# Result stage of a selective-scan kernel in batches: eight weights-block matmuls, then eight 64-row state matmuls

## Chip, core and metric

One NeuronCore of a Trainium2 chip runs the whole program. The metric is the device time of one execution in microseconds (us), as the median of several runs. TensorE does matmuls and transposes, VectorE (DVE), ScalarE (ACT) and GpSimd (POOL) do the elementwise work, SyncE (SP) issues most DMAs and GpSimd the indexed ones. All data are 32-bit floats. The engines run side by side and wait for each other by semaphores.

## What is computed

The input x has 16 images of 256 channels by 32 x 32 = 1024 tokens. Two blocks are added to it. The first scales channels by a small gating network. The second, cut to what matters:

```python
xz = silu(in_proj_w @ gn(x) + in_proj_b)            # 768 rows: x_ssm, res, gate
xf = silu(conv1d_depthwise_3(x_ssm) + dw_b)
dbc = dbc_w @ xf + dbc_b                            # per head: dt, B (8), C (8)
x_h, dt, B_t, C_t = gather by perm[head]            # the head's own order of tokens
# for each token t, S = 8 states per channel:
h = exp(dt_t * A) * h + (dt_t * B_t) * x_t
y_t = sum_s h * C_t   + D * x_t
y = gather back; y = y * silu(gate) + res
x = x + silu(out_proj_w @ y + out_proj_b)
```

There are 2 heads of 128 channels.

## The kernel before

**Tiling and stages.** The images are taken two at a time (NB = 2), so there are PH = 8 phases, written as cycle(i, ...) on every engine. The tokens of a head are cut into 8 tiles of 128 (g = 0 to 7), each of 8 chunks of 16 tokens. The scan isn't run token by token. Inside a chunk it becomes a matmul with a 128 x 128 block of weights (mblk, one for each image and tile), and across chunks a short scan on VectorE gives the state in front of each chunk (hs). The result of a tile is a sum of two matmuls into one PSUM region: the weights block times the gathered rows (x_rows), contraction over 128 rows, here called the weights-block matmul; and the turned C factors times the turned states, contraction over the 64 rows of 8 chunks by 8 states, here called the state matmul.

**The result stage on TensorE.** results(i, h, ...) makes the result of head h for both images. It works in units k = 0 to 7, four for each image b, each of two tiles (e = 0 and 1). turn(i, h, k, ...) transposes cblk and hs for the two tiles at once into PSUM (tp), so that the first tile's state operands come to rows 0 to 63 and the second's to rows 64 to 127. ScalarE copies them to ch (four slots of two times 128 columns, line L570) and signals t_drained. result(i, h, k, ...) waits for that copy and issues four matmuls: weights-block (L1256) and state (L1258) of tile 0 into bank pj[2b], then the same of tile 1 into pj[2b + 1]. The turns run AHEAD = 2 units in front. In head 0 the chunk sums of head 1's first image (st, L1230) are called after unit 3 (between). An f32 matmul is recorded as two weight loads and two matmuls, so 16 + 16 matmuls of a call are 32 + 32 records.

**What stands around it.** TensorE, in a phase: gate matmuls, chunk sums of head 0, the projection of the next phase's first image (project, L1183), results of head 0, the second image's projection mixed with the next phase's rows (L1204, L1206), chunk sums of head 1's second image, results of head 1, rows of the next phase's second image with residual matmuls, turning back, output (L1304). ScalarE runs its own fixed order: turned(...) makes the copies to ch, result(...) copies four tiles per bank from pj to rs (L580) once ch_used says that an image's four units are done, and in head 1 the activation of xf (convolved, L526) stands between the rs copies of the first image and copies 6 and 7. VectorE makes cblk (L1030, after head 0's turns), the scans hs (L995), the weights blocks mblk (L1038 to L1049) and the convolution (L933). GpSimd weighs (L413), gathers head 0's result back in 8 indexed DMAs (L401, once all scans are done), scatters the next phase's rows (L389) and in between gathers head 1's. SyncE stores rs, loads the scattered rows, stores and loads the C rows, stores the output and loads x.

Of the kernel before, what the change touches and what calls it, by code (L numbers as in the profile page):

```python
# [23 lines left out]
P = 128  # L24
# [5 lines left out]
NB = 2  # L30
# [45 lines left out]
def build(nc, x_d, w1g_d, b1g_d, w2_d, b2_d, inw_d, inb_d, dww_d, dwb_d, dbcw_d, dbcb_d, alog_d,  # L76
          dpar_d, mob_d, outw_d, outb_d, const_d, out_d):
    with ExitStack() as ctx:
        def sb(name, width, dt=F32):
            return ctx.enter_context(nc.sbuf_tensor(name, [P, width], dt))  # L80
# [14 lines left out]


        cst = sb("cst", CONST_W)
        inw = sb("inw", CT * 3 * C)
# [19 lines left out]
        hs = sb("hs", NB * (NC + 1) * S)  # L118
        ch = sb("ch", 4 * 2 * P)
        gt = sb("gt", NB * CT * N)  # L120
# [81 lines left out]
        X_U, T_U, Y_U = NB * NT, H * NB * NT // 2, NB * H * 2  # L202
        CH = 4
        AHEAD = 2
# [917 lines left out]
        def _(pe):  # L1122
# [96 lines left out]
            def x_rows(h, b, g):  # L1219
                return v(xp, (h * NT + g) * ROW + b * P, (1, P))  # L1220
# [22 lines left out]

            def result(i, h, k, before):

                b, gp = divmod(k, 4)
                u = h * 8 + k

                if gp == 0:
                    pj_slot(2 * b + 1, None, None, before)  # L1250
                    pe.wait_ge(mblk_ready, i * H + h + 1)
                pe.wait_ge(t_drained, i * T_U + u + 1)
                for e in range(2):
                    g = 2 * gp + e
                    d = v(pj[2 * b + e], gp * P, (1, P))
                    nc.tensor.matmul(d, v(mblk, (b * NT + g) * P, (1, P)), x_rows(h, b, g), start=True, stop=False)  # L1256
                    half_rows = dict(parts=64, p0=64 * e)
                    last = nc.tensor.matmul(d, v(ch, (u % CH) * 2 * P, (1, P), **half_rows),  # L1258
                                            v(ch, (u % CH) * 2 * P + P, (1, P), **half_rows), start=False, stop=True)
                last.then_inc(ch_used, 1)  # L1260

            def results(i, h, before_t, before_r, turned_before=0, between=None):
                for k in range(turned_before, AHEAD):
                    turn(i, h, k, before_t)
                for k in range(8):
                    if k + AHEAD < 8:
                        turn(i, h, k + AHEAD, before_t)
                    result(i, h, k, before_r)
                    if k == 3 and between:
                        between()  # L1270

# [166 lines left out]
```

## Time and profile before

| | |
|---|---|
| median of 3 runs | 1252.72 us (1245.59 to 1258.89) |
| span of the profiled execution, first to last instruction | 1174.1 us |
| TensorE matmul busy | 961.5 us (82%), 3988 instructions |
| VectorE busy | 588.0 us (50%) |
| ScalarE busy | 579.1 us (49%) |
| GpSimd busy | 532.4 us (45%) |
| weights-block matmuls L1256 | 512 records, 120.1 us busy |
| state matmuls L1258 | 512 records, 129.2 us busy |
| mean granted clock of TensorE | 0.890 |

The times of the runs are whole executions; the profile covers one execution from its first to its last instruction, and the time of that execution itself isn't given. Busy time of TensorE counts a matmul from its start to its modelled end, and neighbours overlap, so what a matmul takes of the engine is better read from the distance between starts. The granted clock is 1.00 at 2.4 GHz and 0.50 at 1.2 GHz.

### The profile page before, as it was taken

The page shows a single profiled execution, that of the slowest core. Times are in us where ns is not written, and L with a number is a line of the kernel's source. Part 1 is how long each engine was busy: PE and PEld are TensorE (multiplying, and loading weights), DVE is VectorE, ACT ScalarE, POOL GpSimd, SP SyncE. Part 2 cuts the span into 40 slices and gives each one's busy share as a digit, 9 for nine tenths or more (in the row PEclk, how much of TensorE's full clock was granted, in tenths as well). Part 3 has the DMA queues.
Part 4 walks back from the last instruction along what each step waited for, and adds up shares of the span by engine and source line. Part 5 has one row for each costly group of instructions (what it writes and reads, how often), then busy time and mean ns, then how long its engine had stood idle before and what let it go on. Part 6 is the DMA issues. An engine that isn't in the chain of part 4 may idle for free.

```text
span 1174.1 us, 12950 instructions
## 1 busy us (share of the span) xinstructions
PE 961.5 (82%) x3988; PEld 597.9 (51%) x3988; DVE 588.0 (50%) x1104; ACT 579.1 (49%) x1078; POOL 532.4 (45%) x628
## 2 busy tenths in 40 slices
PE   1039666997899988998899779997999889978966
PEld 0035445664467445754476346744575357634643
DVE  5966136534572448444753348243853466345613
ACT  4824423345734564547444564456553754456341
POOL 0002527164555627371826545471936373644340
PEclk9558765798899998999899989998999899998987
DMA  8830290135912391247513491238313661348122
GB/s 331 331 120 1 81 157 1 36 119 155 216 36 93 101 226 71 72 133 183 140 37 121 144 213 48 78 101 192 121 63 122 179 162 37 119 152 148 37 94 86
DMA packets 112051, 142.54 MB, mean 121 GB/s; under 512 B 41705, under 2 KB 91122, under 8 KB 111986
## 3 DMA queue, kind: packets, MB, share of 16 engines
q1 hardware_dynamic: 99698, 105.91, 34.0%
q0 software_dynamic: 12288, 35.80, 9.4%
q8 instruction: 36, 0.59, 0.2%
q14 instruction: 29, 0.24, 0.1%
HBM read 88.07 MB, written 53.61 MB: 121 GB/s over the span
## 4 chain that ended last, share of the span: by engine, by line
PE 41%; DMA 21%; POOL 16%; issue 10%; DVE 5%; SPq 4%; ACT 3%; POOLq 0%; ACTq 0%; DVEq 0%
PE pj L1183 12%; POOL xt_scratch L389 10%; PE pj L1258 9%; PE pj L1256 8%; DMA xb<-in_x 7%; DMA cd_scratch<-xp 6%; POOL big L401 4%; SPq L302 4%; PE st L1230 3%; DMA xp<-xt_scratch 2%; DMA xt_scratch<-stage,idx 2%; PE tp L1241 2%; PE tp L1206 2%; DMA crow<-cd_scratch 2%; POOL big L413 2%
## 5 line engine op out<-in xcount | busy, mean ns | idle before, releaser
L1183 PE MATMUL pj<-xb,wsc 128*128 128x512 f32 x768 | 392.1, 658 | 39.0 <-DMA xb<-in_x 26.6
L413 POOL TENSOR_TENSOR big<-big,crow 128x128 f32<-128x128 f32 x256 | 182.1, 751 | 212.6 <-DMA crow<-cd_scratch 199.1
L1183 PEld LDWEIGHTS pj<-xb,wsc 128*128 128x128 f32 x768 | 155.0, 213 | 205.9 <-issue 197.7
L389 POOL DMA_INDIRECT xt_scratch<-stage,idx x128 | 139.6, 1091 | 83.0 <-DVE stage L941 46.4
L358 POOL TENSOR_SCALAR wsc<-inw,pcur 128x256 f32<-128x256 f32 x96 | 62.6, 669 | 239.1 <-PE pj L1183 150.7
L401 POOL DMA_INDIRECT big<-yt_scratch,idx x128 | 130.5, 1020 | 75.5 <-issue 37.7
L1258 PE MATMUL pj<-ch 64*128 64x128 f32 x512 | 129.2, 333 | 0.0
L1256 PE MATMUL pj<-xp,mblk 128*128 128x128 f32 x512 | 120.1, 318 | 4.2 <-ACT xs L519 4.2
L1304 PE MATMUL pj<-gt,outw 128*128 128x512 f32 x256 | 111.8, 594 | 0.1
L995 DVE TENSOR_TENSOR_SCAN hs<-big,st 128x64 f32<-128x64 f32 x256 | 49.0, 265 | 101.8 <-PE st L1230 101.8
L570 ACT COPY ch<-tp 128x256 f32<-128x256 f32 x128 | 45.4, 376 | 106.6 <-PE tp L1242 106.6
L1258 PEld LDWEIGHTS pj<-ch 64*128 64x128 f32 x512 | 78.6, 192 | 32.6 <-issue 3.6
L1256 PEld LDWEIGHTS pj<-xp,mblk 128*128 128x128 f32 x512 | 80.0, 197 | 25.1 <-ACT xs L519 4.6
L559 ACT COPY stage<-tp 128x256 f32<-128x256 f32 x128 | 48.0, 375 | 81.4 <-PE tp L1206 77.0
L933 DVE SCALAR_TENSOR_TENSOR xf<-xs,small,xf 128x1024 f32<-128x1024 f32 x64 | 86.1, 1356 | 3.1 <-POOL xf L425 1.4
L1059 DVE TENSOR_TENSOR gt<-tp,gt 128x512 f32<-128x512 f32 x64 | 41.7, 687 | 90.3 <-PE tp L1294 90.0
L941 DVE TENSOR_TENSOR stage<-stage,small 128x68 f32<-128x68 f32 x64 | 14.8, 231 | 134.4 <-ACT stage L560 133.4
L1304 PEld LDWEIGHTS pj<-gt,outw 128*128 128x128 f32 x256 | 48.2, 191 | 58.1 <-issue 57.7
L1230 PEld LDWEIGHTS st<-bblk,xp 128*128 128x128 f32 x512 | 66.0, 205 | 21.2 <-issue 20.1
L580 ACT COPY rs<-pj 128x512 f32<-128x512 f32 x64 | 34.4, 589 | 85.8 <-PE pj L1258 85.8
L1230 PE MATMUL st<-bblk,xp 128*128 128x64 f32 x512 | 66.9, 288 | 8.8 <-DVE bblk L1021 8.8
L547 ACT ACTIVATE big<-sg,small 128x400 f32<-128x400 f32 x128 | 63.9, 610 | 19.6 <-POOL big L413 16.9
(192 smaller groups left out, 1348.7 us busy)
## 6 DMA issues: line engine op xcount, KB each, us to landing
xb<-in_x SPq DMA_DIRECT2D x32, 1024.0 KB, 7.4
xp<-xt_scratch SPq DMA_DIRECT2D x8, 2048.0 KB, 10.0
crow<-cd_scratch SPq DMA_DIRECT2D x128, 128.0 KB, 7.8
yt_scratch<-rs SPq DMA_DIRECT2D x16, 1024.0 KB, 4.4
out<-xb SPq DMA_DIRECT2D x16, 1024.0 KB, 10.2
xp<-xt_scratch SPq DMA_DIRECT2D x8, 272.0 KB, 3.5
xt_scratch<-stage,idx POOLq DMA_INDIRECT x128
big<-yt_scratch,idx POOLq DMA_INDIRECT x128, 2.7
```

The costliest lines, as they stand in the source:

```text
L358: last = nc.gpsimd.tensor_scalar(v(wsc, (b * CT + ct) * 2 * C + slot * C, (1, C)), v(inw, ct * 3 * C + col, (1, C)), v(pcur, (par * NB + b ...
L389: pool.indirect_dma_start(out=xt_d.ap(), out_offset=bass.IndirectOffsetOnAxis(ap=idx[:, k:k + 1], axis=0), in_=v(stage, (nt * H + h) * ROW ...
L401: pool.indirect_dma_start(out=v(big, k * NB * P, (1, NB * P)), out_offset=None, in_=yt_d.ap()[0:(h + 1) * N], in_offset=bass.IndirectOffse ...
L413: last = nc.gpsimd.tensor_tensor(v(big, W_OFF + (s * Q + b * NT) * L, (L, NT), (1, L)), v(big, s * EEW + SEG + b * NT * L, (L, NT), (1, L) ...
L547: last = nc.scalar.activation(v(big, s * EEW, (1, EEW)), v(sg, 0, (1, EEW)), ACT.Exp, scale=v(small, ANEG + h * S + s, (1, 1)))
L933: nc.vector.scalar_tensor_tensor(dst, tap(k), wt(k), dst, ALU.mult, ALU.add).then_inc(conv_step[ot], 1)
L995: nc.vector.tensor_tensor_scan(v(hs, (b * (NC + 1) + 1) * S + s, (S, NC)), v(big, s * EEW + TOT + b * NC, (1, NC)), v(st, s, (S, NC)), 0.0 ...
L1183: last = nc.tensor.matmul(o[:, :], v(wsc, (b * CT + ct) * 2 * C + slot * C + ot * P, (1, P)), x_view(par, b, ct, nt * HALF, HALF), start=( ...
L1230: last = nc.tensor.matmul(v(st, g * CPT * S, (1, CPT * S)), x_rows(h, b, g), v(bblk, (b * NT + g) * CPT * S, (1, CPT * S)), start=True, st ...
L1256: nc.tensor.matmul(d, v(mblk, (b * NT + g) * P, (1, P)), x_rows(h, b, g), start=True, stop=False)
L1258: last = nc.tensor.matmul(d, v(ch, (u % CH) * 2 * P, (1, P), **half_rows), v(ch, (u % CH) * 2 * P + P, (1, P), **half_rows), start=False, ...
L1304: last = nc.tensor.matmul(o[:, :], v(outw, h * C + ot * P, (1, P)), v(gt, (b * CT + h) * N + nt * HALF, (1, HALF)), start=(h == 0), stop=( ...
```

## The change

The two kinds of result matmuls are issued in batches. For each image: the weights-block matmuls of tiles 0 to 3, the turns of units 2 and 3 (6 and 7), the weights-block matmuls of tiles 4 to 7, then the eight state matmuls, in which the rows alternate between 0 to 63 and 64 to 127, and the banks between pj[2b] and pj[2b + 1]. Turns 4 and 5 come after the first image's state matmuls, and between() after them. As all four regions of a bank are now open at once, the start flag is set only for the first matmul into each bank, and the others add to a cleared bank. The constant CH (4) is only moved to where ch is allocated. The wait for mblk and for the banks stands in front of an image's first weights-block matmul as before; the wait for the copies stands in front of the state matmuls.

```diff
@@ -1241,33 +1241,42 @@
                 nc.tensor.transpose(v(o, 0, (1, P)), v(cblk, (b * NT + 2 * gp) * CPT * S, (1, P)), const("ident"))
                 nc.tensor.transpose(v(o, P, (1, P)), v(hs, (b * (NC + 1) + 2 * gp * CPT) * S, (1, P)), const("ident")).then_inc(t_full, 1)
 
-            def result(i, h, k, before):
-
-                b, gp = divmod(k, 4)
-                u = h * 8 + k
-
-                if gp == 0:
+            def within(i, h, b, tiles, before):
+
+                if tiles[0] == 0:
                     pj_slot(2 * b + 1, None, None, before)
                     pe.wait_ge(mblk_ready, i * H + h + 1)
-                pe.wait_ge(t_drained, i * T_U + u + 1)
-                for e in range(2):
-                    g = 2 * gp + e
-                    d = v(pj[2 * b + e], gp * P, (1, P))
-                    nc.tensor.matmul(d, v(mblk, (b * NT + g) * P, (1, P)), x_rows(h, b, g), start=True, stop=False)
-                    half_rows = dict(parts=64, p0=64 * e)
-                    last = nc.tensor.matmul(d, v(ch, (u % CH) * 2 * P, (1, P), **half_rows),
-                                            v(ch, (u % CH) * 2 * P + P, (1, P), **half_rows), start=False, stop=True)
-                last.then_inc(ch_used, 1)
+                for g in tiles:
+                    gp, e = divmod(g, 2)
+                    nc.tensor.matmul(v(pj[2 * b + e], gp * P, (1, P)), v(mblk, (b * NT + g) * P, (1, P)), x_rows(h, b, g),
+                                     start=(gp == 0), stop=False, skip_group_check=True)
+
+            def from_states(i, h, b):
+
+                for gp in range(4):
+                    u = h * 8 + b * 4 + gp
+                    pe.wait_ge(t_drained, i * T_U + u + 1)
+                    for e in range(2):
+                        half_rows = dict(parts=64, p0=64 * e)
+                        last = nc.tensor.matmul(v(pj[2 * b + e], gp * P, (1, P)), v(ch, (u % CH) * 2 * P, (1, P), **half_rows),
+                                                v(ch, (u % CH) * 2 * P + P, (1, P), **half_rows), start=False, stop=True,
+                                                skip_group_check=True)
+                    last.then_inc(ch_used, 1)
 
             def results(i, h, before_t, before_r, turned_before=0, between=None):
-                for k in range(turned_before, AHEAD):
+                for k in range(turned_before, 2):
                     turn(i, h, k, before_t)
-                for k in range(8):
-                    if k + AHEAD < 8:
-                        turn(i, h, k + AHEAD, before_t)
-                    result(i, h, k, before_r)
-                    if k == 3 and between:
-                        between()
+                for b in range(NB):
+                    within(i, h, b, range(0, 4), before_r)
+                    turn(i, h, 4 * b + 2, before_t)
+                    turn(i, h, 4 * b + 3, before_t)
+                    within(i, h, b, range(4, 8), before_r)
+                    from_states(i, h, b)
+                    if b == 0:
+                        turn(i, h, 4, before_t)
+                        turn(i, h, 5, before_t)
+                        if between:
+                            between()
 
             def gate(i, par, units, before):
                 for k in units:
```

## Rows read from the trace of the kernel before

**Rows 1.** The page's chain of waits that ended last, share of the span by line.

```profile
PE pj L1183 12%; POOL xt_scratch L389 10%; PE pj L1258 9%; PE pj L1256 8%; DMA xb<-in_x 7%; DMA cd_scratch<-xp 6%; POOL big L401 4%; SPq L302 4%; PE st L1230 3%; DMA xp<-xt_scratch 2%; DMA xt_scratch<-stage,idx 2%; PE tp L1241 2%; PE tp L1206 2%; DMA crow<-cd_scratch 2%; POOL big L413 2%
```

**Rows 2.** Chain of waits, one phase: start us, us, what.

```profile
429.15 14.99 DMA xb<-in_x
...
444.36 8.79 PE pj L1183 x16
...
498.14 0.43 PE pj L1258 x2
...
501.32 0.29 POOL xt_scratch L389
...
531.85 3.37 DMA xt_scratch<-stage,idx
```

**Rows 3.** Timeline, TensorE, head 0: start us, us, engine line op out<-in xcount.

```profile
452.99 0.27 PE L1241 MATMUL tp<-cst,cblk 128*128 128x128 f32 x1
...
453.21 0.39 PE L1256 MATMUL pj<-xp,mblk 128*128 128x128 f32 x2
453.53 0.49 PE L1258 MATMUL pj<-ch 64*128 64x128 f32 x2
453.94 0.49 PE L1256 MATMUL pj<-xp,mblk 128*128 128x128 f32 x2
454.36 0.48 PE L1258 MATMUL pj<-ch 64*128 64x128 f32 x2
...
460.30 2.00 PE L1230 MATMUL st<-bblk,xp 128*128 128x64 f32 x16
462.14 0.28 PE L1241 MATMUL tp<-cst,cblk 128*128 128x128 f32 x1
...
469.10 3.70 PE L1183 MATMUL pj<-xb,wsc 128*128 128x512 f32 x8
```

**Rows 4.** Timeline, TensorE, head 1 and what follows it.

```profile
483.10 0.28 PE L1241 MATMUL tp<-cst,cblk 128*128 128x128 f32 x1
...
483.95 0.33 PE L1241 MATMUL tp<-cst,cblk 128*128 128x128 f32 x1 [0.24 <-ACT ch L570]
...
498.49 0.44 PE L1204 MATMUL tp<-cst,xf 128*128 128x128 f32 x2
```

**Rows 5.** Timeline, ScalarE, in head 1.

```profile
491.58 1.07 ACT L580 COPY rs<-pj 128x512 f32<-128x512 f32 x2 [1.10 <-PE pj L1258]
492.54 2.19 ACT L526 ACTIVATE xf<-xf,small 128x1024 f32<-128x1024 f32 x2
494.63 0.64 ACT L570 COPY ch<-tp 128x256 f32<-128x256 f32 x2
```

**Rows 6.** Timeline, VectorE, from the second half of head 0 on.

```profile
464.40 1.23 DVE L1030 TENSOR_TENSOR cblk<-bc,cst 128x1024 f32<-128x1024 f32 x1 [3.66 <-PE tp L1242]
465.54 1.53 DVE L995 TENSOR_TENSOR_SCAN hs<-big,st 128x64 f32<-128x64 f32 x8
...
473.60 2.29 DVE L1049 TENSOR_TENSOR mblk<-m,cst 128x2048 f32<-128x2048 f32 x1
...
484.83 5.10 DVE L933 SCALAR_TENSOR_TENSOR xf<-xs,small,xf 128x1024 f32<-128x1024 f32 x4
```

**Rows 7.** Timeline, GpSimd: first and last of eight gathers, first scatter.

```profile
485.75 1.24 POOL L401 DMA_INDIRECT big<-yt_scratch,idx  x1 [0.88 <-DVE hs L995]
...
494.83 0.95 POOL L401 DMA_INDIRECT big<-yt_scratch,idx  x1 [0.30 <-issue]
501.32 0.99 POOL L389 DMA_INDIRECT xt_scratch<-stage,idx  x1 [5.55 <-DVE stage L941]
```

**Rows 8.** Windows: stretch, us, busy (x) of PE, PEld, DVE, ACT, POOL, clock, DMA, GB/s.

```profile
186.60:214.82 28.22, 28.14 (x90) 20.99 (x90) 19.63 (x23) 2.94 (x7) 14.43 (x18) 0.50 0.00 1
...
326.80:342.90 16.10, 16.10 (x94) 12.23 (x92) 12.68 (x17) 3.88 (x9) 10.80 (x12) 1.00 0.00 1
...
218.00:222.00 4.00, 4.00 (x19) 2.31 (x18) 0.00 (x0) 0.70 (x4) 0.00 (x0) 0.87 0.51 172
```

## What the change does to the time, predicted

> **What bounds the kernel now.** I read the chain of waits first. Of the span it gives 9% and 8% to the two matmul lines of the result stage, the state matmuls (L1258) and the weights-block matmuls (L1256) [rows 1]. One phase of the eight, in order of time, shows where they sit: the load of x lands at 444.14 us, the projection starts, and from there to the last state matmul at 498.14 the chain never leaves TensorE except for one short copy (the wait at 483.95 [rows 4]). Then come ScalarE's copies, and GpSimd's scatters from 501.32 to 531.85 us, whose last one feeds the loads of the next phase [rows 2]. So a microsecond taken from TensorE between 444 and 498 us should be a microsecond of the phase, provided that ScalarE, VectorE and GpSimd can start earlier by as much; that I check below.
>
> The second view is TensorE's timeline inside this stretch. I call one run of results(i, h) a half stage; there are 16 (8 phases, 2 heads). Head 0 lasts from 452.99 to 469.10 us, 16.11 us, chunk sums (460.30 to 462.14) included [rows 3]. Head 1 lasts from 483.10 to 498.49, 15.39 us [rows 4]. TensorE is called busy all the time, but look at the starts. An f32 matmul is recorded as two instructions (x2). A turn and its partner start 0.11 us apart (452.99, then the first result matmul at 453.21 after two of them), and sixteen chunk-sum instructions take 1.84 us, 0.115 each. Yet a state matmul holds the engine from 453.53 to 453.94 and the next weights-block matmul from 453.94 to about 454.36: 0.417 us for two instructions that need 2 x 0.107 = 0.214 us [rows 3]. **Each change between a 128-row matmul and a 64-row matmul therefore costs about 0.20 us** in which nothing streams (I read it as the load of new weights and the emptying of the array; the records don't split it). A half stage has 32 of them: 6.5 of its 16 us.
>
> **The change, part by part.** Nothing is removed from the work: each half stage keeps 16 weights-block and 16 state matmuls, 8 pairs of transposes and 8 copies. No DMA and nothing in the queues of SyncE or GpSimd moves. Only the order on TensorE changes.
>
> 1. Sorting. A half stage is now two batches (images), each with 8 weights-block matmuls (two turns in their middle, also of 128 rows) and then 8 state matmuls. The changes of height fall from 32 to 4. Weights-block matmuls behind one another cost 0.107 an instruction, by the turns and chunk sums, which are of the same 128 rows and weight columns. For state matmuls behind one another, on alternating halves of the rows, the trace has no row, since each now stands between two 128-row ones. The nearest rows bound it: at worst as now, 0.417 each; at best two neighbours run beside one another, 0.107 each. I take 0.214, the spacing of all other neighbours: what costs 0.20 now is found exactly at a change of height, and the weights of each instruction are 128 columns wide, which no pair in the trace loads faster than 0.107.
>    Head 0: 64 instructions x 0.107 = 6.85; 12 turns x 0.11 = 1.32; chunk sums 1.83; 4 changes x 0.20 = 0.80; sum 10.8 against 16.1: **5.3 us saved**. Head 1: 6.85 + 16 x 0.11 + 0.80 = 9.4 against 15.4 (which has some 0.5 of waiting for copies, now covered by four weights-block matmuls): **6.0 saved**.
>    The Trainium skill, page TensorEngine Tiling (Array Packing), section Key Properties, says that changing the tiling mode drains TensorE while changing the tile within a mode does not. The trace's 0.20 us per change agrees with the first half; of the second it shows nothing.
>
> 2. Later turns. The state matmuls of a batch wait for four copies made by ScalarE, 0.64 us for two [rows 5]. In batch one, 0.86 us of weights-block matmuls follow the third and fourth turn, and two copies and the signals around them take about 0.8: covered; if that cover were gone, some 0.4 us a batch. The costly place is head 1, second batch. ScalarE's queue is: copies 4 and 5, two rs copies (1.07), two activations of xf (2.19), then copies 6 and 7 (0.64) [rows 5]. The activations need VectorE's convolution, which ends 6.8 us after the half stage starts (484.83 + 5.10 - 483.10) [rows 6]. My times from the half stage's start: state batch one ends at 4.4, turns 4 and 5 at 5.0, copies 4 and 5 at 5.6, rs copies at 6.7, activations at 8.8, copies 6 and 7 at 9.4. TensorE is at state matmul 6 of the second batch at 8.1, and so waits until about 9.1; it ends at 10.0 where it would end at 9.1 to 9.4. **Cost 0.9 us** in the phases that convolve (seven); bounds 0 (if copies come as they do now) and 2.2 (all of the activations exposed). Queued behind the waiting matmul are the rows of the next phase, and behind them the scatters.
>
> 3. Do the others follow? The half stage's blocks of head 1 (mblk) are ready at 475.9 [rows 6], TensorE now wants them at 478: VectorE's last step before them waits for turn 7 of head 0, which comes 3.6 us earlier, so cblk, now at 464.40, starts about 460.8, and 1.2 of cblk, 1.5 of scans and 8.9 of token weights make it about 472.5. Covered by 5 us. GpSimd's gathers of head 0 start at 485.75 behind the scans that follow the chunk sums, and end at 495.8 [rows 7]; they move by head 0's 5.3 us to 490.5. The scatters start at 501.3 and want to move by 10.4 to 490.9. Covered by 0.4 us: just enough. Anything beyond 10.8 us a phase would be cut here.
>
> 4. The first phase. Its head 0 runs at granted clock 0.50 and takes 28.2 us [rows 8]. Doubled instructions give 20.0 + about 1.2 for changes = 21.2: saves 7.0 instead of 5.3. The clock rose only in the projection behind it, 0.87 in 218 to 222 us [rows 8], a run of matmuls without changes of height. The batches are such a run as well, so it may rise inside the half stage: worth between 0 and 7 us (21.2 down to 14, three or four us of it at the low clock). I take 4, a little above the middle, since the engine's instructions come twice as densely as now.
>
> Sum: 8 x (5.3 + 5.1) = 83.2; the first phase 1.7 more and 4 for its clock; the last phase, without convolution, 0.9 more: **89.8 us**. The profiled span of 1174.1 would become 1084. The median of the runs, 1252.72, has 78.6 us outside that span, which the change doesn't touch, so the sum goes off the median: 1252.7 - 89.8 = **1163 us**.
>
> **The rivals.**
> A. The forecast: sorting removes the changes, state matmuls are spaced like all others. 1163; own range 1154 to 1176 (the clock's term at 0 or 7, the stall at 0 or 2.2 in seven phases). Chance 0.50.
> B. Neighbouring state matmuls run beside one another, as their row halves and banks differ. A state batch falls from 1.71 to 0.86. Head 0 saves 7.0; head 1 is then held by ScalarE's queue (copies 6 and 7 end near 8.7, the stage near 9.1) and saves 6.3. The gathers move by 7.0 to 488.8, the scatters want 488.0, so GpSimd takes 1.1 back: 12.2 a phase, 97.6 + 1.7 + 4: 1150. For it: operands in disjoint partitions. Against it: no pair of instructions in the trace beats 0.107. Chance 0.20. (The Trainium skill, same page and section, states that different tiles can execute weight loads and matmuls in parallel; by that rule B is what happens. No row here shows it.)
> C. A state matmul still pays after another state matmul, because the weights of the other half aren't loaded ahead. At 0.417 each, head 0 is 3.42 + 6.67 + 1.32 + 1.83 + 0.4 = 13.6 and saves 2.5, head 1 12.2 and 3.1: 45 + 2 gives 1206. If only the load is exposed (about 0.31, half way), some 66 saved and 1186. Chance 0.23, most of it near the lower price.
> D. Slower: the clock falls in the batches. A half stage at 0.50 is 21.2 against 16.1 now, 5 us lost where 5.3 is won at full clock; it decides once more than half of the 16 are cold, and in all of them the kernel would be at about 1310. Against it: the clock is 1.00 in the result stages after the first one, with the present gaps [rows 8], and batches have fewer. Chance 0.03.
> E. It gives no time because something ends last that I take for covered (GpSimd's gathers, the convolution). GpSimd alone would leave head 0's 5.3 a phase, so only both heads held by others brings it within 1%. Chance 0.04.
>
> **How the numbers follow.** About 1% (12.5 us) is what a measurement of this kernel can tell from no change. A, B and C are all faster by more: 0.93; E 0.04 within; D 0.03 slower. The range takes A whole, B, and C up to a little under its full price: 1146 to 1200. Left out are the dearer end of C (0.08), D, E and a tail of B (0.05), 2 in 10 together.
>
> **What would show it.** In the timeline of TensorE the weights-block instructions should start 0.107 apart, eight state matmuls should last 1.7 us (B: 0.9; C: 2.5 to 3.3), and a half stage of head 0 about 10.8 us. In the waits, a state matmul of head 1 should wait for the ScalarE copy, about 0.9 us, seven times. The scatters should start right behind the gathers, with under 1 us between instead of 5.5. The clock of the first result stage decides term 4. I am wrong if state neighbours cost other than 0.214, or if the gap between gathers and scatters stays wide while the phase doesn't shrink.

## The result, and the profile after

The changed kernel takes 1154.3 us (median of 4 runs, 1147.46 to 1167.46) where the kernel before takes 1255.33 on the same chip: a ratio of 0.919, 95% interval 0.914 to 0.925. The ratio leaves out the slowest run of the changed kernel (1167.46), in which the granted clock was 0.846 for 0.853 to 0.860 in the others. The change is worth 101 us, 8%; 1163 was predicted, and the range holds the time.

TensorE's timeline of the kernel after: the first phase's head 0 (from 185.33), head 1 of a middle phase (331.58 to 340.63) and head 0 in the phase behind it (439.35 to 448.44). The columns are those of [rows 3].

```profile
185.33 2.05 PE L1251 MATMUL pj<-xp,mblk 128*128 128x128 f32 x8 [14.58 <-DVE mblk L1049]
187.18 0.42 PE L1241 MATMUL tp<-cst,cblk 128*128 128x128 f32 x1
...
188.03 1.59 PE L1251 MATMUL pj<-xp,mblk 128*128 128x128 f32 x8
189.55 1.16 PE L1261 MATMUL pj<-ch 64*128 64x128 f32 x16
190.64 0.33 PE L1241 MATMUL tp<-cst,cblk 128*128 128x128 f32 x1
...
196.33 1.98 PE L1183 MATMUL pj<-xb,wsc 128*128 128x512 f32 x4
...
331.58 0.28 PE L1241 MATMUL tp<-cst,cblk 128*128 128x128 f32 x1
...
338.25 0.71 PE L1261 MATMUL pj<-ch 64*128 64x128 f32 x8
339.94 0.77 PE L1261 MATMUL pj<-ch 64*128 64x128 f32 x8 [0.97 <-issue]
340.63 0.44 PE L1204 MATMUL tp<-cst,xf 128*128 128x128 f32 x2
...
439.35 1.05 PE L1251 MATMUL pj<-xp,mblk 128*128 128x128 f32 x8
440.24 0.27 PE L1241 MATMUL tp<-cst,cblk 128*128 128x128 f32 x1
...
441.66 1.16 PE L1261 MATMUL pj<-ch 64*128 64x128 f32 x16
442.75 0.33 PE L1241 MATMUL tp<-cst,cblk 128*128 128x128 f32 x1
...
448.44 1.98 PE L1183 MATMUL pj<-xb,wsc 128*128 128x512 f32 x4
```

Read the starts. Eight weights-block instructions take 0.89 us (439.35 to 440.24), 0.111 each, where the forecast had 0.107. Sixteen state instructions (eight matmuls), up to the next turn, take 1.09 us (441.66 to 442.75), where [rows 3] have 0.417 us for one matmul and the forecast had 0.214. A change of height shows in the single starts as two distances of about 0.2 instead of 0.11, the one at the change and the one behind it; between 441.66 and 442.75 stand the second of the change to 64 rows and the first of the change back, together one change of 0.20. What is left is 0.89 for eight matmuls, 0.111 each. Head 0 lasts 9.09 us instead of 16.11, head 1 9.05 instead of 15.39. That is rival B, to 0.1 us. The 0.97 us at 339.94 is the stall that the prediction put at 0.9; it is there in all seven phases that convolve, 0.97 us each time. The profile gives it no releaser, but ScalarE's timeline has the two copies that this state matmul needs starting at 339.51, right behind the activations:

```profile
339.51 0.65 ACT L570 COPY ch<-tp 128x256 f32<-128x256 f32 x2
```

The individual starts inside one state batch of the kernel after, read from the records (us), come in pairs, one instruction of each row half (the weight loads do too):

```
334.35 334.35 | 334.56 334.56 | 334.67 334.68 | 334.78 334.79
334.89 334.90 | 335.00 335.01 | 335.12 335.12 | 335.23 335.24
```

The window over the first phase's head 0 (columns as in [rows 8]) has a granted clock of 0.83 where [rows 8] have 0.50, and 11.00 us where they have 28.22. By its two parts the clock is 0.50 up to 189.10 and 1.00 from there:

```profile
185.33:196.33 11.00, 11.00 (x92) 10.52 (x92) 10.75 (x12) 3.02 (x8) 11.00 (x13) 0.83 0.01 2
```

**Something that the profile of before did not show.** The waits of the kernel after, grouped by engine, line and what was waited for (us in total, times, longest):

```profile
DVE gt L1059 <- remote: 94.0, 16, 13.3
ACT stage L559 <- remote: 54.9, 16, 6.6
```

And its chain that ended last, by engine:

```profile
PE 44%; issue 14%; another core or an unknown queue 13%; DMA 9%; DVE 8%; ACT 7%; SPq 3%; POOL 1%; POOLq 0%; ACTq 0%; DVEq 0%
```

"Remote" on one core: the profile finds no releaser at that moment, since the TensorE instruction that gives the signal had ended over 1.5 us before. The timeline of TensorE, ScalarE, GpSimd and VectorE in that phase, in order of time:

```profile
334.24 1.24 POOL L401 DMA_INDIRECT big<-yt_scratch,idx  x1 [0.89 <-DVE hs L995]
...
342.93 1.07 ACT L580 COPY rs<-pj 128x512 f32<-128x512 f32 x2 [2.77 <-remote]
...
347.51 0.99 POOL L389 DMA_INDIRECT xt_scratch<-stage,idx  x1 [3.25 <-DVE stage L941]
...
360.75 0.66 PE L1303 MATMUL tp<-cst,big 128*128 128x128 f32 x4 [2.00 <-issue]
...
365.86 0.37 ACT L559 COPY stage<-tp 128x256 f32<-128x256 f32 x1 [5.17 <-remote]
...
376.74 0.96 POOL L389 DMA_INDIRECT xt_scratch<-stage,idx  x1 [0.31 <-issue]
...
379.84 0.69 DVE L1059 TENSOR_TENSOR gt<-tp,gt 128x512 f32<-128x512 f32 x1 [13.26 <-remote]
```

The last state matmul ends at about 340.7, but ScalarE's rs copies of it start at 342.93. Later ScalarE waits 5 us for transposes into stage and VectorE 13 us for those back. The first four of the latter end at 361.4, and VectorE starts on them at 379.84: their signal is 18.4 us late. Of the signals, only TensorE's are late (the count stands with quiet_rows below). The ends of matmuls are modelled, so the trace can't tell a late signal from a late last write; TensorE's next instructions start as usual. From 334.24 to 377.7 GpSimd issues its indexed DMAs almost without a pause. The kernel before has this too, only the profile of [rows 1 to 8] does not: it caught an execution with a span of 1174.1 us, where all timed runs take 1244 to 1270. The experiments take this up.

### The profile page after: what moved, and what is told of

Its sections match the earlier page's. It is cut to its first block, busy times and chain, and to the rows that moved or that the text cites. A ratio compares the mean times of both kernels' runs of the same rounds, so it can differ in the third digit from the quotient of the medians.

```text
span 1154.0 us, 12950 instructions
## 1 busy us (share of the span) xinstructions
PE 850.5 (74%) x3988; PEld 540.1 (47%) x3988; DVE 592.2 (51%) x1104; ACT 574.9 (50%) x1078; POOL 531.5 (46%) x628
## 4 chain that ended last, share of the span: by engine, by line
PE 44%; issue 14%; another core or an unknown queue 13%; DMA 9%; DVE 8%; ACT 7%; SPq 3%; POOL 1%; POOLq 0%; ACTq 0%; DVEq 0%
PE pj L1183 17%; DMA xb<-in_x 6%; PE pj L1313 5%; PE pj L1251 4%; PE st L1230 4%; SPq L302 3%; PE tp L1206 3%; PE pj L1261 2%; PE tp L1204 2%; PE tp L1303 2%; ACT big L547 2%; DVE rs L771 1%; PE tp L1241 1%; PE tp L1242 1%
## 5 line engine op out<-in xcount | busy, mean ns | idle before, releaser
L413 POOL TENSOR_TENSOR big<-big,crow 128x128 f32<-128x128 f32 x256 | 194.0, 797 | 279.4 <-DMA crow<-cd_scratch 195.6
L389 POOL DMA_INDIRECT xt_scratch<-stage,idx x128 | 125.1, 977 | 71.1 <-issue 36.0
L401 POOL DMA_INDIRECT big<-yt_scratch,idx x128 | 124.7, 975 | 65.9 <-issue 37.1
L358 POOL TENSOR_SCALAR wsc<-inw,pcur 128x256 f32<-128x256 f32 x96 | 70.2, 749 | 173.9 <-DVE pcur L916 87.8
L1303 PE MATMUL tp<-cst,big 128*128 128x128 f32 x256 | 48.1, 335 | 131.5 <-DVE gt L1059 65.7
L1059 DVE TENSOR_TENSOR gt<-tp,gt 128x512 f32<-128x512 f32 x64 | 42.3, 688 | 156.6 <-remote 94.0
L1303 PEld LDWEIGHTS tp<-cst,big 128*128 128x128 f32 x256 | 36.0, 170 | 152.9 <-DVE gt L1059 69.9
L618 ACT ACTIVATE rs<-pj,pcur 128x512 f32<-128x512 f32 x56 | 36.5, 692 | 136.5 <-PE pj L1183 88.4
L1204 PE MATMUL tp<-cst,xf 128*128 128x128 f32 x256 | 57.1, 308 | 33.3 <-ACT stage L560 20.4
L1251 PE MATMUL pj<-xp,mblk 128*128 128x128 f32 x512 | 69.6, 280 | 14.6 <-DVE mblk L1049 14.6
L1206 PEld LDWEIGHTS tp<-dbcw,xf 128*128 128x128 f32 x512 | 73.8, 208 | 0.0
L547 ACT ACTIVATE big<-sg,small 128x400 f32<-128x400 f32 x128 | 63.9, 610 | 19.9 <-POOL big L413 17.2
```

The lines of the kernel that those rows point to most:

```text
L389: pool.indirect_dma_start(out=xt_d.ap(), out_offset=bass.IndirectOffsetOnAxis(ap=idx[:, k:k + 1], axis=0), in_=v(stage, (nt * H + h) * ROW ...
L401: pool.indirect_dma_start(out=v(big, k * NB * P, (1, NB * P)), out_offset=None, in_=yt_d.ap()[0:(h + 1) * N], in_offset=bass.IndirectOffse ...
L413: last = nc.gpsimd.tensor_tensor(v(big, W_OFF + (s * Q + b * NT) * L, (L, NT), (1, L)), v(big, s * EEW + SEG + b * NT * L, (L, NT), (1, L) ...
L547: last = nc.scalar.activation(v(big, s * EEW, (1, EEW)), v(sg, 0, (1, EEW)), ACT.Exp, scale=v(small, ANEG + h * S + s, (1, 1)))
L1204: nc.tensor.transpose(v(o, ct * P, (1, P)), tile(ct), const("ident"))
L1206: last = nc.tensor.matmul(v(o, 2 * P, (1, H * K1)), tile(ct), v(dbcw, ct * H * K1, (1, H * K1)), start=(ct == 0), stop=(ct == CT - 1))
```

## The experiments

Times are compared as ratios to the kernel before on the same chip. "First gather" is the start of GpSimd's gathers of head 0 in a middle phase.

**The kernel before, again.** It asks where the 78.6 us between span and median are.

> The kernel before, unchanged, for a second profile. The first profile of it has a span of 1174.1 us though the runs take 1245 to 1259, while the runs of the changed kernel are only 1.8 us longer than their spans; and the changed kernel's trace has waits of up to 13 us (VectorE and ScalarE, releaser unknown) during GpSimd's gathers and scatters that the first trace of before lacks. Theory A: the timed runs of before have such waits too, some 78 us in all, and the first profile was of a lucky execution; then most runs have spans near 1250, and a profile taken now shows either 1174 again or the waits. Theory B: before never has them and its 78 us lie outside the span; then every span is near 1174 with the same times.

Measured: 1264.58 us, ratio 0.999 (0.997 to 1.002). The span of this profile of the unchanged kernel:

```profile
core 0: 1259.5 us, clock 0.858
```

And the longest of its waits that have no releaser in the profile:

```profile
DVE gt L1059 <- remote: 118.3, 11, 16.2
```

The time of that run is 1261.3, so only 1.8 us lie outside the span. My sentence that 78.6 us lie outside it was wrong: they are waits inside, which [rows 1 to 8] don't have. In the execution of those rows TensorE's signals are prompt: in the midst of GpSimd's gathers a copy into stage and the first multiplication are released by TensorE itself, the multiplication 25.4 us behind the first gather (511.19 - 485.75).

```profile
506.44 0.99 POOL L401 DMA_INDIRECT big<-yt_scratch,idx  x1 [0.30 <-issue]
...
508.34 0.37 ACT L559 COPY stage<-tp 128x256 f32<-128x256 f32 x1 [1.92 <-PE tp L1206]
...
511.19 1.29 DVE L1059 TENSOR_TENSOR gt<-tp,gt 128x512 f32<-128x512 f32 x2 [1.50 <-PE tp L1294]
```

**One row half first.** Do the halves make the gain?

```diff
-                for gp in range(4):
...
-                    for e in range(2):
+                for e in range(2):
+                    for gp in range(4):
...
```

> The changed kernel, but in a state batch the four matmuls of rows 0 to 63 (bank 2b) come first and then the four of rows 64 to 127 (bank 2b+1): batches stay, alternation goes. Theory A (neighbours on different row halves run beside one another): a state batch, 1.09 us from its first start to the next turn in the changed kernel, becomes 1.8 to 1.9 us (8 x 0.214 plus a change of 0.2, less one neighbour pair). Head 0 then takes 1.6 us longer, and the kernel some 15 to 20 us longer than the changed one, near 1172. Theory B (64-row matmuls behind one another are cheap whatever their half): the batch stays at 1.1 and the time at 1154.

Measured: ratio 0.936 (0.929 to 0.942) against the kernel after's 0.919 and 0.922. TensorE's timeline, a state batch and what follows:

```profile
454.46 1.71 PE L1262 MATMUL pj<-ch 64*128 64x128 f32 x16
456.10 0.33 PE L1241 MATMUL tp<-cst,cblk 128*128 128x128 f32 x1
```

1.64 us instead of 1.09. Most starts are 0.11 apart; where the second half begins, three pairs come within 0.01 of one another, which is why the batch stays below the 1.8 to 1.9 expected. So state matmuls of one half of the rows cost 0.22 us each, about what I had forecast (0.214), and alternation is what halves it.

**One row half first, banks alternating.** Here the result tiles are laid out anew, so that neighbours of one half write different banks; a signal of TensorE to itself stands between the halves. It separates the half from the bank.

```diff
...
-v(pj[2 * b + e], gp * P, (1, P))
+v(pj[2 * b + gp % 2], (gp // 2 * 2 + e) * P, (1, P))
...
```

> The changed kernel, but the four matmuls of rows 0 to 63 come first and then the four of rows 64 to 127 (behind a signal of TensorE to itself), while the banks alternate between neighbours (the tiles are laid out over the two banks by pairs, and the rs copy follows that layout). It parts the two things that the change alternates. Theory A (the row halves make neighbours overlap): the eight instructions of one half start 0.107 us apart, 0.75 us from first to last, as with one bank. Theory B (the banks do it): they start in pairs 0.01 us apart, 0.35 us in all. The time itself, with a wait in each batch, only says that it is slower than the changed kernel: some 1185.

Measured, in one run: 1204.99 us; what counts here is the spacing. TensorE's timeline, a state batch and the projection behind it:

```profile
452.92 2.37 PE L1263 MATMUL pj<-ch 64*128 64x128 f32 x16
455.22 1.12 PE L1184 MATMUL pj<-xb,wsc 128*128 128x512 f32 x2
```

The single starts are 452.92, 453.14, 453.25, 453.36, 453.47 and so on: 0.11 apart, never in pairs, although the banks alternate. Alternating banks alone gives nothing; different row halves are needed. Whether alternating halves into one bank would do was not tried.

**Pairs inside a unit.** The kernel before, with only its four matmuls of a unit sorted into two weights-block and two state matmuls: 16 changes of height instead of 32.

```diff
+                d = [v(pj[2 * b + e], gp * P, (1, P)) for e in range(2)]
+                for e in range(2):
+                    nc.tensor.matmul(d[e], v(mblk, (b * NT + 2 * gp + e) * P, (1, P)), x_rows(h, b, 2 * gp + e), start=True, stop=False)
                 for e in range(2):
...
-                    nc.tensor.matmul(d, v(mblk, (b * NT + g) * P, (1, P)), x_rows(h, b, g), start=True, stop=False)
...
```

> The kernel before with one edit: in a unit the two weights-block matmuls come first, then the two state matmuls (two halves, two banks). Turns and waits stay. 16 changes of height in a half stage instead of 32. Theory A (0.20 us a change, neighbouring halves beside one another): a unit without turns falls from 1.67 to 0.43 + 0.20 + 0.21 + 0.20 = 1.05 us, head 0 from 16.1 to about 11.5, near 70 us off the whole, about 1185. Rival C (a change costs 0.20 but neighbours don't overlap): unit 1.26, head 0 13.2, some 45 us off, about 1210. Rival: the gain is that of the batches as such (waits for copies), then it stays near before.

Measured: ratio 0.932 (0.925 to 0.938). TensorE's timeline, a unit with turns (from 444.97 to 446.21) and one without (452.94 to 454.00):

```profile
444.97 0.33 PE L1241 MATMUL tp<-cst,cblk 128*128 128x128 f32 x1
...
446.21 0.33 PE L1241 MATMUL tp<-cst,cblk 128*128 128x128 f32 x1
...
452.94 0.71 PE L1255 MATMUL pj<-xp,mblk 128*128 128x128 f32 x4
...
454.00 0.71 PE L1255 MATMUL pj<-xp,mblk 128*128 128x128 f32 x4
```

A unit without turns takes 1.06 us: four weights-block instructions at 0.111 (0.44), four state instructions in pairs at 0.111 (0.22), two changes of 0.20 (0.40); sum 1.06. Both prices hold in a second arrangement. Pairs alone bring most of the gain, since a unit then has two changes of height instead of four, and its two state matmuls already overlap.

**Copies ahead of the activations.** The kernel after, with ScalarE's copies 6 and 7 of head 1 before its two xf activations. What this experiment and the next are held against is a repeat of the kernel after:

> The changed kernel, unchanged, on the chip of the three runs beside it, so that they can be compared with it. About 0.919 of the kernel before. Its trace should again have TensorE's signals late during GpSimd's indexed DMAs (in the first trace the copy of rs starts 2.2 us behind the last state matmul of head 1), as the second profile of the kernel before has (VectorE waiting 15.6 us), and 1.8 us between span and time.

Measured: ratio 0.922 (0.917 to 0.928).

```diff
                 result(i, 1, 0)
+                turned(i, 1, range(4 + AHEAD, 8))
                 if more:
                     convolved(i + 1, 1)
-                turned(i, 1, range(4 + AHEAD, 8))
```

> The changed kernel, but in head 1 ScalarE makes copies 6 and 7 before the two activations of xf, not behind them. Theory A (the stall of 0.97 us ahead of state matmul 6 is only a place in which ScalarE's queue shows, since the rows behind need xf as well): the stall goes, the state batch ends a microsecond earlier, but the first row then waits for xf, and the time stays within 3 us of the changed kernel. Theory B (the prediction's term: the stall costs 0.9 us in seven phases): 6 us less.

Measured: ratio 0.926 (0.920 to 0.932), no gain. TensorE's timeline, last state batch of head 1 and the next rows:

```profile
473.14 1.16 PE L1261 MATMUL pj<-ch 64*128 64x128 f32 x16
475.11 0.44 PE L1204 MATMUL tp<-cst,xf 128*128 128x128 f32 x2 [0.81 <-ACT xf L526]
```

The state batch runs through, and the same wait (0.81 us for 0.97) stands one step later, at the rows that need the activations. ScalarE's queue is the bound of head 1, as step 2 had it; the order of copies and activations in it isn't.

**One signal a batch.** Are TensorE's signals late because it gives so many?

```diff
-                    last.then_inc(ch_used, 1)
+                last.then_inc(ch_used, 4)
```

> The changed kernel, but TensorE signals ch_used once for a state batch (by 4) instead of four times (by 1). Nobody needs the single steps: turns 4 and 5 come behind the batch anyway. Theory A: while GpSimd issues indexed DMAs, TensorE's signals are let through one at a time, some 1.4 us apart (218.71, 220.15, 221.59, 223.01 us in the first trace of the changed kernel), so the three signals fewer in head 1's second batch bring the rs copy and the rows forward by 2 to 4 us a phase: 15 to 30 us less than the changed kernel. Theory B: the signals are late because of what else goes on at that time, whatever their number: no change (under 3 us).

Measured: ratio 0.915 (0.905 to 0.924), not to be told from the repeat's 0.922. ScalarE's timeline has the wait as before:

```profile
466.40 1.07 ACT L580 COPY rs<-pj 128x512 f32<-128x512 f32 x2 [2.74 <-remote]
```

The number of signals is not the cause. The Trainium skill, page TensorE: Matmul & The Clock Gate, section The cost: per-tile semaphore tail, prices one increment at 26 ns; lateness of 2 to 18 us is another thing, and no run here shows the 26 ns.

**Gathers of the last phase later.** In the kernel after, the last state matmul of the whole run is in the batch that starts at 1103.05 and ends at 1104.2, but the copies start at 1110.05, when the eight gathers (1098.60 to 1108.4) are over. Here those gathers wait for the copies.

```diff
+                    if last_phase(i):
+                        pool.wait_ge(r_drained, R_U * (i + 1))
```

> The kernel after; in the last phase only, GpSimd's eight gathers of head 0 wait until ScalarE has made the rs copies of head 1. In the kernel after the last state matmul of that phase ends at 1104.1 us and the second pair of rs copies starts only at 1110.05, when the eight gathers (1098.60 to 1108.41) are over. Theory A (TensorE's signals are late because GpSimd is issuing indexed DMAs): the copies start within 0.5 us of the last state matmul, 5.5 us earlier than now relative to it. Theory B (the signals of a batch are late whatever GpSimd does): the copies still start some 6 us behind the last state matmul. The total time hardly moves in either case, since the sixteen gathers now stand behind the copies (A: 0 to 1 us faster; B: 6 slower).

The timeline of this kernel's last phase, TensorE, ScalarE and GpSimd:

```profile
1126.96 1.16 PE L1263 MATMUL pj<-ch 64*128 64x128 f32 x16
...
1128.17 1.07 ACT L582 COPY rs<-pj 128x512 f32<-128x512 f32 x2 [1.36 <-PE pj L1263]
...
1129.51 1.02 POOL L403 DMA_INDIRECT big<-yt_scratch,idx  x1 [21.24 <-ACT rs L582]
```

The same batch, the same copies, and now 0.05 us between them (1128.12 to 1128.17) instead of 5.8: with GpSimd quiet the signal is prompt. That is theory A, shown in one place. The gathers' transfers are away from that moment too, so issuing and what is issued aren't told apart. (The time, 1177.79 in one run, says nothing more.)

**Three places to be quiet.** The kernel after, each with one added wait of GpSimd, in every phase but the last. quiet_rows: until all next rows stand in stage, before the gathers of head 1.

```diff
                     scatter(i + 1, range(0, 2))
+                if more:
+                    pool.wait_ge(stage_ready, (i + 2) * NT)
                 gather(i, 1)
```

quiet_back: at the same place, until VectorE has multiplied the four halves of head 0 (L1059). pause_scatter: the same wait, behind the gathers of head 1.

```diff
+                    pool.wait_ge(y_drained, i * Y_U + 4)
```

> The kernel after; in each phase but the last GpSimd waits, before the gathers of head 1, until all eight tiles of next rows stand in stage. In the kernel after those gathers start at 352.63, and the last copies into stage, whose transposes TensorE issued by 356.8, come late at 360.23 and 365.86. Theory A (signals late while GpSimd issues): the last copy comes at about 357.5, GpSimd starts its queue about 5 us later and ends it 5 us later, at about 383; the gate's activation and the transposes back move about 8 us earlier, but their own signals are then late in turn, so the phase gains or loses up to 3 us: 1135 to 1180. Theory B (late for another cause): the last copy stays at 365, and GpSimd loses 13 us a phase: 1240.

> The kernel after; in each phase but the last GpSimd waits, before the gathers of head 1, until VectorE has multiplied the four halves of y of head 0 (turned back by TensorE). In the kernel after TensorE stands still from 367.5 to 380.59 for these multiplications. Theory A (signals late while GpSimd issues): the fourth multiplication ends near 364 where it now ends near 383, TensorE's next projections move up by 15 us, and GpSimd's queue ends 11 us later, at 389. TensorE gains more than GpSimd loses: 0 to 6 us a phase faster, 1110 to 1158; if the row loads behind the scatters end last, up to 11 us a phase slower (1235). Theory B (late for another cause): the multiplications come no sooner, GpSimd waits 25 us a phase: 1330.

> The kernel after; in each phase but the last GpSimd waits between the gathers of head 1 and the last twelve scatters until VectorE has multiplied the four halves of y of head 0. The gathers of head 1 still end at 362.5, with the transposes' signals late until then. Theory A (signals late while GpSimd issues): once GpSimd pauses at 362.5 the late signals arrive at once, stage is complete at 363, the gate's activation ends at 365, the four multiplications near 368 instead of 383; TensorE's projections come 14 us earlier, GpSimd's queue ends 5.5 us later, at 383. 3 to 8 us a phase faster: 1098 to 1133. Theory B (late for another cause): no multiplication comes sooner, and GpSimd loses 20 us a phase: 1290.

Measured: ratios 0.888 (0.884 to 0.892), 0.910 (0.906 to 0.913) and 0.908 (0.904 to 0.912). A wait more, and all three are faster than the kernel after. Of the first, the timeline of ScalarE, GpSimd and VectorE:

```profile
359.98 0.37 ACT L561 COPY stage<-tp 128x256 f32<-128x256 f32 x1 [0.15 <-PE tp L1208]
...
361.56 0.98 POOL L401 DMA_INDIRECT big<-yt_scratch,idx  x1 [4.71 <-DVE stage L943]
...
362.22 1.29 DVE L1061 TENSOR_TENSOR gt<-tp,gt 128x512 f32<-128x512 f32 x2 [1.50 <-PE tp L1305]
...
386.40 0.96 POOL L389 DMA_INDIRECT xt_scratch<-stage,idx  x1 [0.30 <-issue]
```

The copies follow their transposes at 0.15 us, and the first multiplication comes 24.5 us after the first gather (337.71), where the kernel after has 45.6 (379.84 - 334.24). GpSimd's last scatter starts 48.7 us after the first gather instead of 42.5, 6 us later, and the phase is shorter all the same. Theory B (late for another cause) expected slower kernels in all three. Of A's sizes only quiet_back's was met (1147.54 for 1110 to 1158; its fourth multiplication ends at 364.3 where 364 was expected). The others were missed: quiet_rows beat its range (1120 for 1135 to 1180), since the multiplications too came promptly though GpSimd was issuing again, and pause_scatter fell short of its own (1144 for 1098 to 1133): its first multiplication comes 31.4 us after the first gather, its last scatter 51.2.

The records of the semaphores say the same of the whole span. Of TensorE's signals in quiet_rows (759), 107 are recorded more than 0.07 us behind the end of an instruction that gives them, and 105 of these 107 lie inside a run of GpSimd's indexed DMAs or within 3 us behind one, although such runs fill only 324 of 1120 us. In the kernel after it is 87 of 104. No recorded signal of ScalarE or VectorE is that late in any run (some, 75 and 23 in the kernel after, have no record at all), and in the execution of [rows 1 to 8] none of TensorE's is, with the same queue on GpSimd.

**GpSimd's queue in bursts.** In quiet_rows the last rs copies still start at 349.32, 5 us behind their state matmuls (344.1), under the gathers of head 0. So the queue is cut once more:

```diff
...
-                gather(i, 0)
+                gather(i, 0, range(0, 5))
+                pool.wait_ge(r_drained, R_U * (i + 1))
                 if more:
                     scatter(i + 1, range(0, 2))
+                gather(i, 0, range(5, NT))
+                if more:
+                    pool.wait_ge(stage_ready, (i + 2) * NT)
                 gather(i, 1)
```

> The kernel with the wait of e9_quiet_rows, and GpSimd's queue cut once more: five gathers of head 0, then a wait for the rs copies of head 1, the first four scatters, the other three gathers of head 0, the wait for all tiles in stage, and the rest as before. In e9_quiet_rows the last rs copies start at 349.32 though their state matmuls end at 344.1, since the gathers run from 337.71 to 347.7; the first scatter starts at 352.05 and the last ends at 387.4, and the chain runs from it over the row loads to the next phase. Theory A (signals late while GpSimd issues): the fifth gather ends at 343.9, the rs copies start near 344.3, the first scatter near 347, and the last ends 3 to 6 us earlier than in e9_quiet_rows; in the last phase some 5 us more. 1077 to 1101, ratio 0.856 to 0.873. Theory B (the gain of e9_quiet_rows came from something else, such as fewer transfers at one time): the copies stay at 349, and three gathers more stand behind them: the same as e9_quiet_rows or up to 4 us a phase slower, 1120 to 1146.

Measured: 1096.44 us (1095.36 to 1103.98, 6 runs) against 1264.65, ratio 0.870 (0.867 to 0.873). The timeline of ScalarE, GpSimd and VectorE:

```profile
340.38 1.07 ACT L585 COPY rs<-pj 128x512 f32<-128x512 f32 x2 [1.53 <-PE pj L1266]
...
343.11 0.99 POOL L389 DMA_INDIRECT xt_scratch<-stage,idx  x1 [3.92 <-DVE stage L946]
...
354.31 1.45 DVE L1064 TENSOR_TENSOR gt<-tp,gt 128x512 f32<-128x512 f32 x2 [1.07 <-PE tp L1308]
...
379.39 0.96 POOL L389 DMA_INDIRECT xt_scratch<-stage,idx  x1 [0.30 <-issue]
```

The copies name TensorE as their releaser again and start 1.0 us behind their last state matmul (339.4), where quiet_rows has 5.2; from the first gather (332.93) to the last scatter it is 46.5 us, to the first multiplication 21.4. This is the best version of the study: the ratio is 5.3 to 5.6% below the kernel after's (0.870 to 0.919 or 0.922), with the same work on every engine: only two waits of GpSimd are added and three of its gathers stand elsewhere.

The mean length of the second to seventh phase, from head 0's first weights-block matmul to the next phase's, from the records of each profiled execution (us):

```
before, execution of rows 1 to 8    127.4
before, again                       140.4
pairs inside a unit                 130.3
after                               128.2
after, again                        129.5
after, quiet_back                   125.8
after, pause_scatter                125.4
after, quiet_rows                   122.0
after, bursts                       119.4
```

## Why the prediction was right, and where it was not

**The price of a change of height, 0.20 us: right.** Pairs inside a unit and the batches both add up with it. (The Trainium skill, page TensorEngine Tiling (Array Packing), Key Properties, has the drain at a change of mode; the runs agree.)

**State matmuls behind one another, 0.214 us each: wrong, the mis-sized term.** They cost 0.111, so by the prediction's own sign ("wrong if state neighbours cost other than 0.214") its account of them fails. I gave B 0.20 because no pair in the trace started closer than 0.107. That holds for instructions of 128 columns only (those of 34 columns, L1206, start 0.03 apart there), and it was no evidence against B: every neighbour in that trace used the same rows of the array, or came behind a change of height, so the trace could not have shown an overlap. With one half at a time my 0.214 is nearly measured (0.22); with halves alternating it is half. The Trainium skill's other rule in that section, that tiles work in parallel, is what happens. The term was worth 1.7 us in head 0 (7.0 saved for 5.3), and 1.2 in head 1 (6.3 for 6.0 less the stall's 0.9), as B had it.

**The stall of 0.9 us in head 1: right**, 0.97 at its place, and moved but not removed by the other order of the copies. Without it head 1 would save some 7.3 us instead of 6.3 (an estimate: 6.34 + 0.97).

**The clock of the first phase: right in kind, too small.** I took 4 of 7 us. Head 0 lasts 11.0 us for 28.2, so 17.2 are saved where 7.0 + 4 were forecast. At half clock throughout, 9.1 us would be 18.2, so the clock gives some 7.2 of the 17.2, and the faster state matmuls the 3 that are left over (estimates from these spans). The eight instructions from 185.33 take 1.85 us, which is half clock; the state batch at 189.55 already takes the 1.09 us of full clock. In the records the clock rises at 189.1, with TensorE in the batches since 185.33; in the kernel with pairs it rises at 190.7, inside the half stage too. Before, with a change at every matmul, it stayed at 0.50 for 28 us [rows 8], in the repeat as well.

**Who follows.** In six phases 12.2 us each are saved (140.4 to 128.2), in the first 26.2, in the last 7.0, less 1.0 by which the first result stage starts later: 105.4, and the spans 1259.5 and 1154.0, of two chips, differ by 105.5. The repeat of the kernel after has 129.5 us a phase, so the 12.2 are known to about 1 us only. The forecast was 10.4, 16.1 and 11.3. 12.2 is B's number, but partly by luck: B has 13.3 less 1.1 for GpSimd's queue. The gap in front of the scatters, to shrink from 5.55 [rows 7] to under 1 us, is 3.25, since the rs copies ahead of them are late by 2.2; no term of the prediction has such a wait. In the last phase head 1 gained next to nothing: TensorE finishes its part over 6 us sooner, now under the gathers, and its last signal waits until they are over (1104.2 to 1110.05).

**The base of the sum: a wrong sentence that did little harm.** "78.6 us outside that span, which the change doesn't touch" is false; they are lateness inside the span. Both kernels carry it, so the difference stayed near the forecast, which is luck: nothing in the prediction says why the change should leave it alone, and in the last phase it didn't. Had I asked what a span of 1174.1 beside a median of 1252.7 means, I would have seen that the rows were of an unusual execution, that some 80 us of waits were missing in them, and that part of these could be had (some 60 us from the kernel after to the bursts).

**Chances.** A was right on the changes of height, with a mis-sized term for the neighbours, and B, at 0.20, was what happened on TensorE: its 1150 against 1154.3 measured. The time also lies at the very end of A's own range (1154 to 1176), which it reaches only with the clock's term at 7 and no stall, though the stall came. C (1186 to 1206) would have been the kernel with neighbours paying as at a change; no run shows such a price. D and E did not occur.

## What to carry to other kernels

Where matmuls of different heights alternate, count the changes: each costs 0.20 us here, sorting them needs no new work, and small-height matmuls should then alternate between the halves of the rows (and, as here, write to two banks), since two of them ran in the time of one. Before taking a span from a profile as the base of a sum, hold it against the run times; here the gap of 6% was waits that this profile didn't have. And a queue of DMA issues on GpSimd is worth cutting where TensorE's signals are on the chain: two waits more, and three gathers moved, made this kernel some 5.5% faster.

## What the hardware showed that I had not expected

- Matmuls on rows 0 to 63 and 64 to 127, alternating, start within 0.01 us of one another and cost 0.111 us a matmul (two recorded instructions), own weights included. On one half it is 0.22 us, also when the banks alternate. Alternating halves with one bank was not tried.
- TensorE's signals arrive late while GpSimd issues indexed DMAs, by 2 us at 340.7 and 18 us at 361.4 in the phase shown, in 13 of the 14 profiled executions. One kernel's two spans are 1174.1 without this and 1259.5 with it, 78 of the 85 us in the six middle phases (127.4 and 140.4 each); the granted clock, 0.890 and 0.858, is part of the difference. No recorded signal of ScalarE or VectorE is late. With GpSimd quiet TensorE's are prompt (0.05 us for 5.8).
- Late signals stand in or just behind runs of such issues (105 of 107 in quiet_rows), but issuing isn't enough: in the execution of [rows 1 to 8], and for the first microseconds of a run of DMAs (quiet_rows from 361.56), signals are prompt while GpSimd issues. What else it takes, and what in the chip holds the signals, stays open; the experiments only moved GpSimd's issues.
